# Four conditional residual layers on one core: preparation of the first pair of blocks moved earlier, and b1s loads issued ahead of output writes

## What is computed

```python
B, T, D = 32, 64, 1024                       # x: (32, 64, 1024) f32
x = x + einsum('bct,bcd->bdt', x, w0[adapter])                 # w0: (16, 64, 64)
x = x + x @ W1 + (x @ A1[adapter]) @ B1[adapter]               # A1: (16, 1024, 16)
x = x + x @ W2.T + 0.5 * (x @ A2[labeler]) @ B2.T              # A2: (5, 1024, 32)
logits = x @ Wr.T + 5.0 * one_hot(language, 8)
topw, topi = top_k(logits, 2); gates = sum(one_hot(topi) * softmax(topw))
x = x + x @ W3.T + 2.0 * einsum('bter,bte,eor->bto', x @ A3, gates, B3)   # A3: (8, 16, 1024)
```

## Time and profile before

| | |
|---|---|
| median of 3 runs | 558.46 us (558.45 to 558.51) |
| the profiled execution's own time | 558.84 us |
| its span, first to last instruction | 556.8 us |
| PE busy | 538.9 us, 97% |
| DVE, ACT, POOL busy | 250.2, 164.6, 166.6 us |
| mean granted TensorE clock | 0.990 of full |

### The profile page before, as it was taken

One profiled execution on the slowest core, in us unless ns is written; L12 is line 12 of the kernel. 1 busy time (PEld: TensorE's weight loads), 2 busy tenths in 40 slices (PEclk: granted clock), 3 DMA queues, 4 the chain that ended last, 5 costly groups with the idle time before them and its releaser, 6 DMA issues.

```text
span 556.8 us, 9108 instructions
## 1 busy us (share of the span) xinstructions
PE 538.9 (97%) x2803; PEld 478.9 (86%) x2803; DVE 250.2 (45%) x614; ACT 164.6 (30%) x318; POOL 166.6 (30%) x251
## 2 busy tenths in 40 slices
PE   8999999999999999999797999999999999999997
PEld 8999999999999999999676788787888878878785
DVE  4751312132311112117597465654756547565463
ACT  5541311121111111117343332333323333233322
POOL 2401000000001002338772444435444344443400
PEclk9999999999999999999798999999999999999999
DMA  8703010045150001020140331313213232132302
GB/s 307 281 1 127 2 75 15 1 165 173 55 179 35 26 27 34 35 80 1 26 159 2 126 98 54 92 77 125 97 52 92 77 125 97 54 91 77 126 16 75
DMA packets 23914, 46.72 MB, mean 84 GB/s; under 512 B 7620, under 2 KB 13124, under 8 KB 23764
## 3 DMA queue, kind: packets, MB, share of 16 engines
q1 hardware_dynamic: 23700, 45.85, 24.5%
q0 software_dynamic: 192, 0.59, 0.3%
HBM read 33.39 MB, written 13.04 MB: 83 GB/s over the span
## 4 chain that ended last, share of the span: by engine, by line
PE 79%; SPq 5%; DVE 5%; DMA 3%; issue 3%; POOL 3%; ACT 1%; POOLq 0%; ACTq 0%; DVEq 0%
PE bank L1262 23%; PE bank L1296 21%; PE bank L1216 20%; PE bank L1282 8%; DMA b1s<-b1scr 3%; SPq L402 2%; PE bank L1344 2%; SPq L418 2%; PE bank L1352 1%; DVE xb_lo L884 1%; DVE ost L1098 1%; ACT xb_hi L751 1%; POOL tr L539 1%; POOL bd_hi L515 1%; PE bank L1306 1%
## 5 line engine op out<-in xcount | busy, mean ns | idle before, releaser
L1262 PE MATMUL bank<-e_lo,w1t_hi 128*128 128x488 f32 (+2 forms) x240 | 86.9, 362 | 0.0
L1262 PE MATMUL bank<-e_hi,w1t_hi 128*128 128x488 f32 (+2 forms) x240 | 86.8, 362 | 0.0
L1262 PE MATMUL bank<-e_hi,w1t_lo 128*128 128x488 f32 (+2 forms) x240 | 86.7, 361 | 0.0
L1216 PE MATMUL bank<-g_hi,w2s_hi 128*128 128x384 f32 (+1 forms) x192 | 65.5, 341 | 0.5 <-DVE w2s_lo L884 0.5
L1216 PE MATMUL bank<-g_lo,w2s_hi 128*128 128x384 f32 (+1 forms) x192 | 65.3, 340 | 0.0
L1216 PE MATMUL bank<-g_hi,w2s_lo 128*128 128x384 f32 (+1 forms) x192 | 65.2, 340 | 0.0
L884 DVE TENSOR_TENSOR w1t_lo<-raw,w1t_hi 128x1024 fp32r<-128x1024 f32 x18 | 23.4, 1302 | 69.7 <-ACT w1t_hi L645 60.0
L1262 PEld LDWEIGHTS bank<-e_lo,w1t_hi 128*128 128x128 f32 x240 | 45.1, 188 | 3.9
L1262 PEld LDWEIGHTS bank<-e_hi,w1t_hi 128*128 128x128 f32 x240 | 45.0, 188 | 4.0
L1262 PEld LDWEIGHTS bank<-e_hi,w1t_lo 128*128 128x128 f32 x240 | 45.1, 188 | 3.9
L884 DVE TENSOR_TENSOR e_lo<-bank,e_hi 128x384 fp32r<-128x384 f32 (+1 forms) x24 | 13.3, 561 | 60.9 <-ACT e_hi L680 60.9
(11 more groups left out here) (204 smaller groups left out, 1276.0 us busy)
## 6 DMA issues: line engine op xcount, KB each, us to landing
raw<-in_x_dram SPq DMA_DIRECT2D x16, 512.0 KB, 3.4
out_dram<-ost SPq DMA_DIRECT2D x32, 256.0 KB, 2.0
b1s<-b1scr SPq DMA_DIRECT2D x32, 217.5 KB, 2.6
raw<-in_b1w_dram SPq DMA_DIRECT2D x10, 512.0 KB, 3.2
w2raw<-in_w_dram SPq DMA_DIRECT2D x7, 512.0 KB, 7.3
graw<-in_w3a3wr_dram SPq DMA_DIRECT2D x4, 768.0 KB, 8.6
graw<-in_w3a3wr_dram SPq DMA_DIRECT2D x8, 196.0 KB, 6.4
b1scr<-b1stage_hi SPq DMA_DIRECT2D x8, 192.0 KB
```

The source lines that it names most:

```text
L1216: ins = nc.tensor.matmul(to[:, 0:w], lhs, G[c][z][:, k, 0:w], start=(k == 0 and n == 0), stop=(k == K - 1 and n == len(terms) - 1), skip_g ...
L1262: ins = nc.tensor.matmul(stage_bank(u, j)[:, 0:WIDTH[c]], W1T[u][a][:, k, :], EX[c][z][:, k, :], start=(k == 0 and (a, z) == TERMS[0]), st ...
```

## The change

It moves work in three places and adds one wait.

- POOL makes the two diagonal matrices and the first sum of x ahead of the combinations of row 6 of M, where before it made them behind these.
- In the first pair DVE makes h2c of block 1 (`second_low_rank(1, 1)`) ahead of `route(0)`, and the sum for p7 ahead of h1c. ACT, DVE and PE are reordered around that: `h2_t` and `left_hi(1)` now stand ahead of `exp_of(0)`, `left_lo(1)` stands right behind `gates(0)`, PE waits for it (s_opl 7) ahead of `h2_into(1, 1)`, and `gated_across(0, 0)` comes behind `narrow(2)`. `gates(1)` gets a wait for that transpose, since it writes gh again.
- In the SP queue each `load_b1s` stands in front of the output write of tile 1 or 3, where it stood behind it. It still waits until PE has finished that tile.

```diff
--- before.py
+++ after.py
@@ -446,6 +446,11 @@
                     for s in range(2):
                         sp.dma_start(raw[s][:, :, :], x[bass.ds(2 * p + 2 + s, 1)].rearrange("a p k t -> p (a k) t")).then_inc(s_raw[s], 16)
                 for n, (s, c) in enumerate(TILES):
+                    if n % 2 and not last:
+                        done = held(sp, 4 * p + n + 1)
+                        sp.wait_ge(s_idx, 48)
+                        sp.wait_ge(s_y, done)
+                        load_b1s(2 * p + 2 + s, s)
                     sp.wait_ge(s_idx, 48)
                     if n % 2 == 0:
                         sp.wait_ge(s_ya, 2 * p + n // 2 + 1)
@@ -453,11 +458,6 @@
                         sp.wait_ge(s_yd, 2 * p + n // 2 + 1)
                     sp.dma_start(orows[bass.ds(2 * p + s, 1)].rearrange("a t d -> (a t) d")[:, c * BANK:(c + 1) * BANK], ost[n][:, :]
                                  ).then_inc(s_st[n], 16)
-                    if n % 2 and not last:
-                        done = held(sp, 4 * p + n + 1)
-                        sp.wait_ge(s_idx, 48)
-                        sp.wait_ge(s_y, done)
-                        load_b1s(2 * p + 2 + s, s)
 
             pair_io(0, False)
             with sp.Fori(1, NP - 1) as p:
@@ -561,21 +561,22 @@
                 nc.gpsimd.tensor_tensor(tmp[:, :, :], raw[1][:, 0:KH, :], raw[1][:, KH:K, :], ALU.add).then_inc(s_sum, 1)
 
             pool.wait_ge(s_b1st, 16 * 12 * LORA)
+            pool.wait_ge(s_idx, 48)
+            pool.wait_ge(s_bdz, 2)
+            pool.wait_ge(s_a1, 16)
+            r11, r12, r21, r22 = [raw[n // 2][:, n % 2 * KH:(n % 2 + 1) * KH, :] for n in range(4)]
             for k in range(K - 1):
+                if k == K - 2:
+                    diagonal(0, 0, 0)
+                    diagonal(1, 1, 0)
+                    pool.wait_ge(s_raw[1], 16 * (ROWS // 2 + 1))
+                    nc.gpsimd.tensor_tensor(sum0[:, :, :], r21, r22, ALU.add).then_inc(s_sum, 1)
                 row_there(k)
                 if k < KH:
                     combine(TR[0][:, k, :], MR[1][:, k, :], MR[0][:, k, :], ALU.subtract)
                 else:
                     for n in (3, 2, 4):
                         right_of(n, k - KH)
-            pool.wait_ge(s_idx, 48)
-            pool.wait_ge(s_bdz, 2)
-            pool.wait_ge(s_a1, 16)
-            r11, r12, r21, r22 = [raw[n // 2][:, n % 2 * KH:(n % 2 + 1) * KH, :] for n in range(4)]
-            pool.wait_ge(s_raw[1], 16 * (ROWS // 2 + 1))
-            nc.gpsimd.tensor_tensor(sum0[:, :, :], r21, r22, ALU.add).then_inc(s_sum, 1)
-            diagonal(0, 0, 0)
-            diagonal(1, 1, 0)
             chosen = choose(0)
             pool.wait_ge(s_acc, ACC_A + ACC_B - 2)
             pool.wait_ge(s_rd, 3 * LAST + 2)
@@ -811,17 +812,17 @@
                 act.wait_ge(s_trd, BACK_SUM["t4"])
                 split_hi("t4", WHOLE)
                 h1_t(1, 1)
+                h2_t(1, 1)
+                left_hi(1)
                 exp_of(0)
                 act.wait_ge(s_wide, PRODUCT["p7"])
                 xm_hi(0, bank[BA])
                 act.wait_ge(s_b3, 16)
                 nc.scalar.activation(B3[0][:, :], b3raw[:, :], ACT.Copy).then_inc(s_b3h, 1)
-                h2_t(1, 1)
-                left_hi(1)
                 act.wait_ge(s_wide, PRODUCT["p3"])
                 xm_hi(1, bank[BD_])
+                exp_of(1)
                 ght_hi(0, 0)
-                exp_of(1)
                 xn_hi(2, YB + 1)
                 ght_hi(1, 1)
                 last_tiles_hi(0)
@@ -1054,7 +1055,7 @@
                 steps.hold()
                 steps.then(V.tensor_copy(topf[:, :], topi[:, 0:2]))
 
-            def gates(b, s, steps):
+            def gates(b, s, steps, read=None):
 
                 nar = bank[RT + s]
                 dve.wait_ge(s_ex, b + 1)
@@ -1069,6 +1070,8 @@
                 steps.hold()
                 steps.then(V.tensor_tensor(gate[:, :], gm[:, 0, :], gm[:, 1, :], ALU.add))
                 steps.hold()
+                if read is not None:
+                    dve.wait_ge(s_tg, read)
                 V.tensor_tensor(gh[:, :, :], nar[:, 0:ER].rearrange("p (e r) -> p e r", e=E),
                                 gate[:, :].unsqueeze(2).to_broadcast([P, E, R3]), ALU.mult).then_inc(s_gh, 1)
 
@@ -1144,20 +1147,20 @@
                 split_lo("b22", WHOLE, SPLIT_HI["b22"])
                 xn_lo(1, YB)
                 operand_lo(XB[1][:, 0:KH, :], tmp[:, :, :], XB[0][:, 0:KH, :], 6)
+                sum_p7(0)
                 first_low_rank(1, 1, steps)
                 split_lo("t4", WHOLE, SPLIT_HI["t4"])
+                second_low_rank(1, 1, steps)
                 route(0, 0, steps)
-                sum_p7(0)
                 gates(0, 0, steps)
-                second_low_rank(1, 1, steps)
+                left_lo(1)
                 xm_lo(0, bank[BA], 1)
                 dve.wait_ge(s_b3h, 1)
                 lo(B3[1][:, :], b3raw[:, :], B3[0][:, :], s_b3l)
-                left_lo(1)
+                route(1, 1, steps)
                 xm_lo(1, bank[BD_], 2)
                 ght_lo(0, 0)
-                route(1, 1, steps)
-                gates(1, 1, steps)
+                gates(1, 1, steps, read=1)
                 xn_lo(2, YB + 1)
                 ght_lo(1, 1)
                 last_tiles_lo(0)
@@ -1384,24 +1387,25 @@
                 pe.wait_ge(s_add, 2)
                 pe.wait_ge(s_opl, 5)
                 there("t3b")
-                part("p7", 0, 6)
+                part("p7", 0, 9)
                 mixed(1, 1)
-                part("p7", 6, 12)
+                part("p7", 9, 12)
                 pe.wait_ge(s_opl, 6)
                 there("b22")
+                part("p3", 0, 4)
                 h1_across(1, 1)
-                part("p3", 0, 6)
+                part("p3", 4, 10)
                 h1_into(1, 1, 0)
-                part("p3", 6, 12)
+                part("p3", 10, 12)
                 pe.wait_ge(s_add, 3)
                 there("t4")
+                part("p4", 0, 6)
                 h2_across(1, 1)
-                part("p4", 0, 8)
+                part("p4", 6, 12)
+                pe.wait_ge(s_opl, 7)
+                h2_into(1, 1)
+                narrow(2, XA, YB + 1)
                 gated_across(0, 0)
-                h2_into(1, 1)
-                part("p4", 8, 12)
-                pe.wait_ge(s_opl, 7)
-                narrow(2, XA, YB + 1)
                 tile(0, 0, True, False)
                 gated_across(1, 1)
                 for n in range(1, 4):
```

## The result

| | before | changed |
|---|---|---|
| median | 558.49 us (4 runs, 558.45 to 559.46) | 600.9 us (4 runs, 598.9 to 602.08) |
| the profiled execution's own time | 558.84 us | 598.9 us |
| its span | 556.8 us | 597.1 us |
| mean granted TensorE clock | 0.990 | 0.959 |

The ratio is 1.0745, with an interval of 1.0724 to 1.0766: slower by 7.4%, 8.9 us above the forecast and inside its range. The profiled execution is the fastest of the four.

The account below looks back on a forecast made before the run. PE, busy for 97% of the span, was taken to bound the kernel. 558.84 − 5.0 (first pair) + 26.6 (waits for h2T) + 11.9 (half clock) = 592.3, as a median 592.0 us; range 576 to 603.

Parts of the forecast that it names:

- The wait of 4.4 us: At h2_into in each of seven pairs, PE waits 4.4 us for h2T, held back by tile 3's late output write.
- The net of 3.8 us a pair: At h2_into, after the b1s wait is gone and with restart, PE goes on 3.8 us later per pair, 26.6 in seven.
- the delay of DS: In each pair, tile 1's later write delays DS by 0.6 us, hidden by the eight matmuls of p5 behind it.
- The clock: Behind each new PE wait at h2_into, half clock costs 1.7 us a pair, 11.9 us for seven.
- the 5.0 us: Gain up to and through the first pair, from moving POOL's block and reordering DVE's list: 5.0 us, bounds 2 and 8.
- rival (c): POOL's block is held up or the wait for XA eats the gain: 0 in place of −5.0, 597 us; 8%.
- part 1: POOL's diagonals and sum ahead of row 6: the 3.4 us wait for s_lo before narrow(0) goes; balance 6.0 us earlier.
- the 6.0 us: Balance at narrow(0) and p6: 3.4 us of wait, 2.8 and 0.3 of half clock saved, some 0.5 of DVE backlog new.
- part 2: First pair, h2c moved up in DVE's list: the 4.0 us wait goes; narrow(2) starts 7.4 us earlier, tiles 4.7.
- The wait for XA: Ahead of narrow(2) in the first pair, PE idles 3.9 us for left_lo(1), queued behind gates(0).
- Rival (a): Tile 3's write does not matter, so the pairs lose nothing and the kernel gets faster: 548 us; 10%.
- 5.4 us for the b1s waits: PE's waits for b1s at the pairs' starts go: 4.4 us over seven pairs, 5.4 with restarts.

## Why the prediction was right, and where it was not

**The sign and the mechanism were right.** The step that decided, b1s[1] standing in front of tile 3's write, held link by link: write, xb_hi, h2T, h2_into. The kernels with and without that one move show it (601.5 and 558.0 us), and so does moving the wait (580.4).

**The wait of 4.4 us** was 3.5 to 4.2, in part since PE comes to it up to 0.5 us late for h2c; with tile 1's write left in its place it was 4.2 on average (29.5 us in seven). The net of 3.8 us a pair measured 4.0 (38.94 − 34.90, with the clock held at full). The sentence that failed is that the delay of DS would be hidden by eight matmuls. It is hidden from p6, but h2c stands behind ds_lo, and h2_across comes one matmul before the end of p5. I had followed the operand to its reader, not the queue behind it.

**The clock**, taken at 1.7 us a pair from the row of the second wait, measured 1.7 by the traces and 2.0 by the medians. By the rule of the Trainium skill that I set against it ("TensorE: Matmul & The Clock Gate", Part 1: under 1% of a typical span) it would be at most 5.6 us in all, an estimate. Filling the waits gave 14.1 us, 2.5% of the span before. The rule speaks of one warming up; here it is paid in every pair, and the measurement decides.

**The moves of the first pair went as told up to narrow(0).** POOL's block, in the gap and beside a mostly idle DVE, took 4.1 us (238.49 to 242.55; 4 to 5 forecast), and take(0) began at 258.50 (258.0 forecast), as POOL's rows of the changed kernel show:

```profile
238.49 0.46 POOL L510 TENSOR_TENSOR bdraw<-bdraw,ident 128x128 f32<-128x128 f32 x1
...
241.26 1.29 POOL L573 TENSOR_TENSOR sum<-raw 128x512 f32<-128x512 f32 x1
...
258.50 1.20 POOL L532 CAST s_hi<-tba 128x256 fp32r x2 [5.61 <-ACT tba L702]
```

**But the 5.0 us did not come**: 0.7 us measured, with an interval that reaches 0. That is rival (c), and it is most of what the forecast missed: the changed kernel's profiled execution took 598.9 us, the sum said 592.3, and 5.0 of the 6.6 between them are this term (tile 2 of the first pair starts at 307.40 us in the changed kernel's trace and at 307.38 in that of the kernel before). Most of the rest is the pairs, 40.3 us measured and 38.5 forecast.

What failed in part 1 is the step behind narrow(0): that half a us of DVE's backlog at `mixed` was all that came back. The wait for s_lo did go, though with 0.8 us in hand and not 2.9, since take(0) took 7.9 us and not 6.3. But PE then waited 2.3 us for ds_lo and 1.1 for xn_lo, and the half clock moved from narrow(0) to p6. In this window of 2 us, 0.50 is the granted clock:

```profile
276.00:278.00 2.00, 2.00 (x6) 1.42 (x5) 1.90 (x4) 0.00 (x0) 2.00 (x4) 0.50 0.74 235
```

narrow(1) started at 281.40 us against 282.37: of the 6.0 us, 1.0 was left. I priced POOL's take by its own row and left DVE's rows as they were, though the row with the inflated cast had shown that a row beside the other engine can be much longer.

What failed in part 2 is that DVE's list "moves as a whole", by those 6 us. It moved by 0.9 (xb_lo ended at 286.7, forecast 281.7), and t4_lo, at 284.0 in the forecast, came later than before:

```profile
289.05 2.52 DVE L885 TENSOR_TENSOR t_lo<-tr,t_hi 128x2048 fp32r<-128x2048 f32 x1
```

The wait for XA was seen (3.9 us forecast, 2.9 measured, half clock behind it: narrow(2) took 4.4 us). The start of narrow(2) was not 7.4 us earlier, but 3.0: in the chain of the changed kernel it stands as

```profile
298.04 4.36 PE bank L1285 x24
```

against 301.02 and 2.67 us before.

**Rival (a)**, the b1s waits gone at no cost, was not what this change did. Its 5.4 us for the b1s waits are, with 6.5 measured, what b1s[0] moved alone gives once the waits for the writes are moved too: 551.8 us.

## What to carry to other kernels

Before a transfer is moved up a queue, list what it now stands in front of, and ask for each who waits for that to land. A write out of a buffer that shares memory with an operand is such a thing, and its waiters queue others behind them. Put each wait on the engine and the part of the buffer that needs it: that alone made the same move gain 1.3% where it had gained 0.3%. The seven waits of PE of 3.5 to 4.2 us were paid for nearly one and a half times (5.75 us a pair), by themselves and by the half clock behind them.

## What was not expected of the hardware

- DVE and POOL slowed each other down far more than I had allowed for. A 128x512 difference on DVE took 0.69 us with POOL idle, up to 1.23 beside POOL's take and 1.78 beside its sum of x; the take took 4.8 us nearly alone and 7.9 beside DVE. The Trainium skill says that GpSimd's interfaces to SBUF are shared with VectorE, and names DVE instructions with two SBUF inputs among those that contend ("GPSIMD Engine Reference", Specifications); these DVE rows, all of that kind, agree.
- The two are not always slowed evenly. In the kernel before, the cast of 128x128 that took 2.39 us ran from 254.54 to 256.93, beside this row of DVE, which ended at 256.78:

```profile
254.49 2.29 DVE L884 TENSOR_TENSOR b_lo<-mr_left,b_hi 128x2048 fp32r<-128x2048 f32 x1 [1.16 <-ACT b_hi L717]
```

In the changed kernel the same row of DVE takes 2.29 us too, with POOL idle. So here POOL bore the whole delay, and the cast looks as if it had waited for DVE's instruction to end; no run tests that.
- Matmuls whose result nobody uses made the changed kernel 14 us faster, by keeping the granted clock at 1.00 through the waits.
